# Attention pass of a graph layer: one load of each step's word per engine, and the words under way kept in registers

## The chip, the cores and the metric

The kernel runs on one core of a Trainium2 chip. The core has five engines that run side by side, each with a queue of instructions of its own: TensorE (PE, matrix products), VectorE (DVE), ScalarE (ACT), GpSimd (POOL) and SyncE (SP, which here only issues transfers). The metric is the device time of one launch in microseconds (us), the median of several.

## The reference, cut to what matters

The whole kernel computes two graph layers on 3125 nodes with 256 features and 50000 edges. The edges are sorted by their target `dst`. The change is in one stage of the first layer, the sum of softmax-weighted values over the edges of a node:

```python
# one row per edge, 4 heads of 64 features
ex  = exp(score - largest_score_of[dst])          # E x 4
num = segment_sum(ex[:, :, None] * v[src], dst)   # N x 4 x 64
den = segment_sum(ex, dst)                        # N x 4
rst = num / den
```

Scores, values of the edges' sources (stored in DRAM as `d_v`) and the largest scores have been made by stages before it.

## The kernel before, in words

Edges are held in tiles of 128 (one edge per partition), nodes in 25 tiles of 128. A list of steps, made at run time from `dst`, pairs a node tile `t` with two neighbouring edge tiles `i` and `i + 1` (`G = 2`) that hold edges of that node tile. A step is one 32-bit word in SBUF, `t << 9 | i` (`PACK = 9`). `step_at(eng, m, s)` loads the word of step `s` into a register of the engine `eng` (`value_load`, line 397) and takes `t` and `i` out of it; addresses that depend on `t` or `i` are worked out by register instructions of the engine's own queue.

`attention_sums` goes through the steps four at a time (`UN = 4` buffers, index `u`); such four steps are a round, and the loop is a `Fori` over rounds. There are 212 steps, so 53 rounds, the last of which stands unrolled behind the loop on ACT and DVE (`last` is the number of rounds in the loop). For step `s = 4 r + u`:

- SP waits until `weigh` of step `s - 4` is done and loads `v[:, u]`, 128 x 512 values (L759).
- ACT makes a one-hot matrix: `distance` writes |node number - dst| for both edge tiles (two `Abs` instructions of 128x128, L771), `one_hot` turns it into 0 and 1 (one `Relu` of 128x256, L777). `distance` of step `s + 1` is issued ahead of `one_hot` of step `s`. `one_hot` waits until PE has finished step `s - 4`.
- DVE `weigh` multiplies `v` with the edge's four weights (L822, 128x512). DVE `keep` adds the finished product of a step from PSUM to the node tile's row of `sums` (L832, 128x260). The order on DVE is `weigh(s + 2)`, `keep(s)`.
- POOL copies the weights themselves beside the weighted values, to be summed too (L806, 128x8); it waits for PE's step `s - 4`.
- PE multiplies one-hot and weighted values of the two edge tiles into PSUM (L863; an fp32 product of two tiles is four passes, so four MATMUL records per step).

So DVE runs two steps ahead of its own `keep`, and ACT, POOL and SP up to four steps ahead of PE. The order of the work is written out by hand with semaphores: `weighted`, `multiplied`, `kept`, `hots`, `copied`, `own`, `arrived[u]`. Both `weigh` and `keep` call `step_at` at their start, so that DVE loads the word of every step twice, two steps apart; ACT, POOL and SP load it once.

Of the kernel before, what the change touches and what calls it, by code (L numbers as in the profile page):

```python
# [11 lines left out]
ACT = mybir.ActivationFunctionType  # L12
AX = mybir.AxisListType

P = 128
# [379 lines left out]
def step_at(eng, m, s):  # L395

    v = eng.value_load(m.steps[0:1, bass.ds(s, 1)])
    why = "the steps are made of tiles that exist"
    t = eng.snap(eng.bass.s_assert_within(v >> PACK, 0, NT - 1, skip_runtime_bounds_check_because=why))
    i = eng.snap(eng.bass.s_assert_within(v & ((1 << PACK) - 1), 0, ET - G, skip_runtime_bounds_check_because=why))  # L400
    return t, i

def last_round(eng, m):
    return eng.value_load(m.rounds[0:1, 1:2], min_val=1, max_val=STEPS // UN - 1)

# [331 lines left out]
def attention_sums(nc, a, m, banks):  # L738

    WIDE = F + HEADS  # L740
    with Stage(nc, "attend") as st:
        v = st.sb("v", [P, UN, G, F])
        pv = st.sb("pv", [P, UN, G, WIDE])
        minus = st.sb("minus", [P, ET])
        far = st.sb("far", [P, UN, G * P])
        hot = st.sb("hot", [P, UN, G * P])
        weighted, multiplied, kept, hots, copied, own = (
            st.sem(x) for x in ("weighted", "multiplied", "kept", "hots", "copied", "own"))
        diff, exps, free = st.sem("diff"), st.sem("exps"), st.sem("free")
        arrived = [st.sem(f"arrived{u}") for u in range(UN)]  # L750
        with nc.Block() as block:
            @block.sync
            def _(sp):
                with sp.Fori(0, rounds_of(sp, m)) as r:
                    for u in range(UN):
                        t, i = step_at(sp, m, r * UN + u)
                        sp.wait_ge(weighted, r * UN + (u + 1))
                        sp.sem_inc(free, 1)
                        sp.dma_start(v[:, u], m.d_v[u][:, bass.ds(i, G), :]).then_inc(arrived[u], 16)  # L759

            @block.scalar
            def _(act):
                act.sem_inc(multiplied, UN)
                act.wait_ge(diff, 3)
                nc.scalar.activation(m.probs[:], m.probs[:], ACT.Exp, scale=float(HD) ** -0.5).then_inc(exps, 1)

                def distance(r, u):
                    t, i = step_at(act, m, r * UN + u)
                    act.wait_ge(hots, r * UN + (u + 1))
                    for g in range(G):  # L770
                        nc.scalar.activation(far[:, u, g * P:(g + 1) * P], m.node_no[:, bass.ds(t * P, P)], ACT.Abs,  # L771
                                             bias=minus[:, bass.ds(i + g, 1)]).then_inc(own, 1)

                def one_hot(r, u):
                    act.wait_ge(own, r * (UN * G) + (G * u + G))
                    act.wait_ge(multiplied, r * UN + (u + 1))
                    nc.scalar.activation(hot[:, u], far[:, u], ACT.Relu, scale=-1.0, bias=1.0).then_inc(hots, 1)  # L777
                last = last_round(act, m)
                t, i = step_at(act, m, 0)
                for g in range(G):  # L780
                    nc.scalar.activation(far[:, 0, g * P:(g + 1) * P], m.node_no[:, bass.ds(t * P, P)], ACT.Abs,
                                         bias=minus[:, bass.ds(i + g, 1)]).then_inc(own, 1)
                with act.Fori(0, last) as r:
                    for u in range(UN):
                        if u + 1 < UN:
                            distance(r, u + 1)
                        else:
                            distance(r + 1, 0)
                        one_hot(r, u)
                for u in range(UN):  # L790
                    if u + 1 < UN:
                        distance(last, u + 1)
                    one_hot(last, u)

            @block.gpsimd
            def _(pool):
                pool.sem_inc(hots, UN)
                pool.sem_inc(weighted, UN)
                pool.sem_inc(kept, UN)
                pool.wait_ge(exps, 1)  # L800
                with pool.Fori(0, rounds_of(pool, m)) as r:
                    for u in range(UN):
                        s = pool.snap(r * UN + u)
                        t, i = step_at(pool, m, s)
                        pool.wait_ge(multiplied, s + 1)
                        nc.gpsimd.tensor_copy(pv[:, u, :, F:WIDE], m.probs[:, bass.ds(i, G), :]).then_inc(copied, 1)  # L806

            @block.vector
            def _(dve):
                nc.vector.tensor_tensor(m.probs[:], m.scores[:].rearrange("p h j -> p j h"), m.probs[:],  # L810
                                        ALU.subtract).then_inc(diff, 1)
                dve.wait_ge(diff, 1)

                nc.vector.tensor_scalar(m.probs[:], m.probs[:], 0.0, None, ALU.min).then_inc(diff, 1)
                nc.vector.tensor_scalar(minus[:], m.dst[:], -1.0, None, ALU.mult).then_inc(diff, 1)
                dve.wait_ge(exps, 1)

                def weigh(r, u):
                    t, i = step_at(dve, m, r * UN + u)
                    dve.wait_ge(arrived[u], r * 16 + 16)  # L820
                    dve.wait_ge(multiplied, r * UN + (u + 1))
                    nc.vector.tensor_tensor(pv[:, u, :, 0:F].rearrange("p g (h d) -> p g h d", h=HEADS),  # L822
                                            v[:, u].rearrange("p g (h d) -> p g h d", h=HEADS),
                                            m.probs[:, bass.ds(i, G), :].unsqueeze(3).to_broadcast([P, G, HEADS, HD]),
                                            ALU.mult).then_inc(weighted, 1)

                def keep(r, u):
                    t, i = step_at(dve, m, r * UN + u)
                    dve.wait_ge(multiplied, r * UN + (u + 1 + UN))
                    dve.wait_ge(kept, r * UN + (u + UN))  # L830
                    at = m.sums[:, bass.ds(t, 1), :]
                    nc.vector.tensor_tensor(at, at, banks[u][:, 0:WIDE].unsqueeze(1), ALU.add).then_inc(kept, 1)  # L832
                last = last_round(dve, m)
                for u in range(2):
                    t, i = step_at(dve, m, u)
                    dve.wait_ge(arrived[u], 16)
                    nc.vector.tensor_tensor(pv[:, u, :, 0:F].rearrange("p g (h d) -> p g h d", h=HEADS),
                                            v[:, u].rearrange("p g (h d) -> p g h d", h=HEADS),
                                            m.probs[:, bass.ds(i, G), :].unsqueeze(3).to_broadcast([P, G, HEADS, HD]),
                                            ALU.mult).then_inc(weighted, 1)  # L840
                with dve.Fori(0, last) as r:
                    for u in range(UN):
                        if u + 2 < UN:
                            weigh(r, u + 2)
                        else:
                            weigh(r + 1, u + 2 - UN)
                        keep(r, u)
                for u in range(UN):
                    if u + 2 < UN:
                        weigh(last, u + 2)  # L850
                    keep(last, u)

            @block.tensor
            def _(pe):
                with pe.Fori(0, rounds_of(pe, m)) as r:
                    for u in range(UN):
                        s = pe.snap(r * UN + u)
                        pe.wait_ge(hots, s + (1 + UN))
                        pe.wait_ge(copied, s + 1)
                        pe.wait_ge(weighted, s + (1 + UN))  # L860
                        pe.wait_ge(kept, s + 1)
                        for g in range(G):
                            mm = nc.tensor.matmul(banks[u][:, 0:WIDE], hot[:, u, g * P:(g + 1) * P], pv[:, u, g],  # L863
                                                  start=g == 0, stop=g == G - 1)
                        mm.then_inc(multiplied, 1)
# [1486 lines left out]
```

## Time and profile before

| | |
|---|---|
| median of 3 runs | 4048.72 us (4047.67 to 4053.07) |
| profiled execution | 4048.99 us |
| its span | 4047.3 us |
| granted TensorE clock, mean of the span | 0.865 |
| busy share of the span | PE 77%, DVE 52%, ACT 29%, POOL 28% |
| attention pass, from the first transfer of `v` to the last `keep` | 860.9 to 1214.0 us |

The times of the table and of all rows come from the one profiled execution, except for the median. Line numbers such as L822 are those of the kernel before.
### The profile page before, as it was taken

What the parts mean: (1) busy time and instruction counts of PE and PEld (TensorE: products, weight loads), DVE (VectorE), ACT (ScalarE), POOL (GpSimd) and SP (SyncE); (2) the same over time, 40 slices, a digit from 0 to 9 for tenths busy, and PEclk for the clock granted to TensorE, in tenths of its full rate; (3) what the DMA queues carried; (4) which work ended last, traced back from release to release, by engine and by line L of the source; (5) the groups of instructions that cost most, each with busy time, mean ns of one, the idle gap of its engine ahead of it and who ended that gap; (6) DMA issues with size and microseconds to landing.
All of it is one profiled execution on the core that took longest, in us unless ns stands there. A gap on an engine that the chain in (4) does not pass through costs nothing. (4 is left out here: it accounts for less than half of the span.)

```text
span 4047.3 us, 64299 instructions
## 1 busy us (share of the span) xinstructions
PE 3103.2 (77%) x12404; PEld 2300.5 (57%) x12405; DVE 2122.8 (52%) x3755; ACT 1177.5 (29%) x2663; POOL 1118.4 (28%) x1227
## 2 busy tenths in 40 slices
PE   4767667736666734999998899999996868666979
PEld 2634434424445433567776788888885656554568
DVE  6466666666663286111113455555556874884231
ACT  1000000036662411233333000000007975653312
POOL 2166666601110000000000355555550001750023
PEclk9866665569998875799999999999998989887979
DMA  1588888835550000000000565556650000004134
GB/s 54 174 268 268 267 265 266 268 87 161 160 151 6 18 0 17 0 16 8 16 8 3 173 176 175 174 178 178 175 175 33 0 19 1 1 0 163 78 128 139
DMA packets 219248, 449.64 MB, mean 111 GB/s; under 512 B 30122, under 2 KB 109299, under 8 KB 217771
## 3 DMA queue, kind: packets, MB, share of 16 engines
q1 hardware_dynamic: 158762, 257.80, 20.7%
q0 software_dynamic: 60416, 190.96, 15.9%
q8 instruction: 39, 0.64, 0.1%
q14 instruction: 31, 0.25, 0.0%
HBM read 360.37 MB, written 89.26 MB: 111 GB/s over the span
## 5 line engine op out<-in xcount | busy, mean ns | idle before, releaser
L1401 POOL DMA_INDIRECT conv_h<-table_h,conv_ix x424 | 409.0, 965 | 1048.4 <-ACT conv_ix L1392 957.8
L1452 PE MATMUL bank<-conv_w,conv_eT 128*128 128x256 f32 x2532 | 580.9, 379 | 0.0
L489 PE MATMUL bank<-scores_k,scores_hotT 128*128 x848 | 391.1, 609 | 183.1 <-DVE scores_hotT L518 177.0
L1452 PEld LDWEIGHTS bank<-conv_w,conv_eT 128*128 128x128 f32 x2532 | 482.1, 190 | 64.5
L467 POOL DMA_INDIRECT scores_qv<-table_qv,scores_ix x424 | 400.9, 946 | 374.0 <-ACT scores_ix L457 160.8
L489 PEld LDWEIGHTS bank<-scores_k,scores_hotT 128*128 128x128 f32 x848 | 225.6, 294 | 331.2 <-issue 299.0
L1351 DVE SCALAR_TENSOR_TENSOR x<-bank,soft_w,x 128x256 f32 x200 | 96.8, 484 | 443.2 <-PE bank L1285 443.2
L863 PE MATMUL bank<-attend_pv,attend_hot 128*128 128x260 f32 x848 | 237.2, 403 | 118.9 <-POOL attend_pv L806 83.0
L1313 ACT ACTIVATE soft_h<-bank,soft_bi,soft_sc 128x320 f32<-128x320 f32 x320 | 197.5, 617 | 340.0 <-PE bank L1278 340.0
L1392 ACT ACTIVATE conv_ix<-src 128x2 int32 x212 | 43.2, 204 | 770.1 <-DVE conv_msg L1426 736.6
L863 PEld LDWEIGHTS bank<-attend_pv,attend_hot 128*128 128x128 f32 x848 | 145.2, 190 | 210.8 <-POOL attend_pv L806 121.9
L1459 PE MATMUL bank<-conv_msg,conv_hot 128*128 128x256 f32 x848 | 223.3, 386 | 44.5 <-DVE conv_msg L1426 44.5
L457 ACT ACTIVATE scores_ix<-src 128x2 int32 x212 | 43.1, 203 | 666.2 <-DVE scores_qk L525 584.6
L525 DVE TENSOR_TENSOR scores_qk<-scores_qv,bank 128x512 f32<-128x512 f32 x212 | 145.7, 687 | 135.7 <-DMA scores_qv<-table_qv,scores_ix 89.8
L1459 PEld LDWEIGHTS bank<-conv_msg,conv_hot 128*128 128x128 f32 x848 | 157.0, 190 | 84.6 <-DVE conv_msg L1426 64.6
L822 DVE TENSOR_TENSOR attend_pv<-attend_v,probs 128x512 f32<-128x512 f32 x210 | 145.5, 693 | 102.4 <-issue 99.1
L167 PE MATMUL bank<-ident,rows 128*128 128x128 f32 x250 | 51.1, 362 | 192.4 <-DVE rows L156 190.8
L1278 PE MATMUL bank<-xT,soft_W 128*128 x640 | 188.4, 444 | 8.0 <-issue 3.7
L1421 DVE TENSOR_TENSOR conv_be<-bank,conv_b 128x512 f32<-128x512 f32 x212 | 145.9, 688 | 91.4 <-PE bank L1452 86.6
L1278 PE MATMUL bank<-soft_h,soft_W 128*128 128x320 f32 x640 | 182.4, 438 | 0.0
L1285 PE MATMUL bank<-soft_W,soft_h 128*128 128x256 f32 x800 | 179.2, 379 | 0.0
L771 ACT ACTIVATE attend_far<-node_no,attend_minus 128x128 f32 x422 | 146.3, 394 | 77.9 <-ACT attend_hot L777 77.6
(420 smaller groups left out, 5250.8 us busy)
## 6 DMA issues: line engine op xcount, KB each, us to landing
conv_eT<-in_edges SPq DMA_DIRECT2D x212, 384.0 KB, 3.3
edge_v<-scores_qv SPq DMA_DIRECT2D x212, 256.0 KB, 4.2
attend_v<-edge_v SPq DMA_DIRECT2D x212, 256.0 KB, 2.7
hidden_rows<-rows SPq DMA_DIRECT2D x25, 512.0 KB, 3.8
top_wd<-in_top_wd SPq DMA_DIRECT2D x8, 1024.0 KB, 11.4
scores_qv<-table_qv,scores_ix POOLq DMA_INDIRECT x424, 4.8
conv_h<-table_h,conv_ix POOLq DMA_INDIRECT x424, 3.3
table_qv<-qkv_rows SPq DMA_DIRECT2D x50, 128.0 KB, 1.7
```

The costliest lines, as they stand in the source:

```text
L467: nc.gpsimd.indirect_dma_start(out=qv[:, u, g - u * G, :], out_offset=None, in_=m.d_qv, in_offset=bass.IndirectOffsetOnAxis(ap=ix[:, g:g + ...
L489: mm = nc.tensor.matmul(banks[u][:, g * F:(g + 1) * F], hotT[:, u, g * P:(g + 1) * P], k[:, bass.ds(t, 1), :].rearrange("p t f -> p (t f)" ...
L525: nc.vector.tensor_tensor(qk[:, u % 2].rearrange("p (g f) -> p g f", g=G), qv[:, u, :, 0:F], banks[u][:, 0:G * F].rearrange("p (g f) -> p ...
L771: nc.scalar.activation(far[:, u, g * P:(g + 1) * P], m.node_no[:, bass.ds(t * P, P)], ACT.Abs, bias=minus[:, bass.ds(i + g, 1)]).then_inc( ...
L863: mm = nc.tensor.matmul(banks[u][:, 0:WIDE], hot[:, u, g * P:(g + 1) * P], pv[:, u, g], start=g == 0, stop=g == G - 1)
L1278: mm = nc.tensor.matmul(banks[k % HSLOTS][:, 0:CW], W[:, j, layer, f, c * P:(c + 1) * P], cols, start=f == 0, stop=f == FT - 1)
L1285: mm = nc.tensor.matmul(banks[HSLOTS + u][:, 0:F], h2[:, f, u * P:(u + 1) * P], W[:, j, 2, f], start=f == 0, stop=f == FT - 1)
L1313: nc.scalar.activation(dst[:, c, hf * CW:(hf + 1) * CW], banks[k % HSLOTS][:, 0:CW], ACT.Relu, scale=sc[:, layer, bass.ds(e, 1), c], bias= ...
L1401: nc.gpsimd.indirect_dma_start(out=h[:, u, g, :], out_offset=None, in_=m.d_h, in_offset=bass.IndirectOffsetOnAxis(ap=ix[:, u * G + g:u * G ...
L1421: nc.vector.tensor_tensor(be[:, u % 2], banks[u][:, 0:G * F].rearrange("p (g f) -> p g f", g=G), b[:].unsqueeze(1).to_broadcast([P, G, F]) ...
L1452: mm = nc.tensor.matmul(banks[u][:, g * F:(g + 1) * F], eT[:, u, g, c], w[:, c], start=c == 0, stop=c == EC - 1)
L1459: mm = nc.tensor.matmul(acc(u), hot[:, u, g], msg[:, u, g], start=g == 0, stop=g == G - 1)
```

## The change

On ACT and DVE `step_at` gives way to three small functions: `word_at` loads a word, `node_tile` and `edge_tile` take `t` and `i` out of a word that is already in a register.

- On DVE the word of a step is loaded once, three steps before its `keep`, between the `weigh` of another step and the `keep` that follows. Three words are under way; at the end of a round they are copied to three registers that live across the loop's branch (`reg_mov`), and at its start they are read back (`snap`).
- On ACT the load of the next step's word moves from ahead of `distance` to between the two `Abs` instructions of a `distance`. `distance` is called once per edge tile and takes `t` and `i` out of the word each time. One word is carried across the branch.
- The order of `weigh`, `keep`, `distance` and `one_hot`, and all semaphores, stay as they were. SP, POOL and PE are untouched.

```diff
+def word_at(eng, m, s):
+    return eng.value_load(m.steps[0:1, bass.ds(s, 1)])
+
+def node_tile(eng, v):
+    return eng.snap(eng.bass.s_assert_within(v >> PACK, 0, NT - 1, ...))
+
+def edge_tile(eng, v):
+    return eng.snap(eng.bass.s_assert_within(v & ((1 << PACK) - 1), 0, ET - G, ...))
...
-                def distance(r, u):
-                    t, i = step_at(act, m, r * UN + u)
-                    act.wait_ge(hots, r * UN + (u + 1))
-                    for g in range(G):
-                        nc.scalar.activation(far[:, u, g * P:(g + 1) * P], ...)
+                def distance(word, u, g):
+                    t, i = node_tile(act, word), edge_tile(act, word)
+                    nc.scalar.activation(far[:, u, g * P:(g + 1) * P], ...)
...
+                def round_of(r, word, more):
+                    for u in range(UN):
+                        if more or u + 1 < UN:
+                            act.wait_ge(hots, r * UN + (u + 2))
+                            distance(word, (u + 1) % UN, 0)
+                            later = word_at(act, m, r * UN + (u + 2)) if more or u + 2 < UN else word
+                            distance(word, (u + 1) % UN, 1)
+                            word = later
+                        one_hot(r, u)
+                    return word
...
                 with act.Fori(0, last) as r:
-                    for u in range(UN):
-                        if u + 1 < UN:
-                            distance(r, u + 1)
-                        else:
-                            distance(r + 1, 0)
-                        one_hot(r, u)
+                    act.reg_mov(carried, round_of(r, act.snap(carried), True))
...
-                def weigh(r, u):
-                    t, i = step_at(dve, m, r * UN + u)
+                def weigh(r, u, word):
+                    i = edge_tile(dve, word)
...
-                def keep(r, u):
-                    t, i = step_at(dve, m, r * UN + u)
+                def keep(r, u, word):
+                    t = node_tile(dve, word)
...
+                def round_of(r, words, more):
+                    for u in range(UN):
+                        if u + 2 < UN:
+                            weigh(r, u + 2, words[u + 2])
+                        elif more:
+                            weigh(r + 1, u + 2 - UN, words[u + 2])
+                        if more or u + 3 < UN:
+                            words.append(word_at(dve, m, r * UN + (u + 3)))
+                        keep(r, u, words[u])
+                    return words[UN:]
...
                 with dve.Fori(0, last) as r:
+                    for x, word in zip(carried, round_of(r, [dve.snap(x) for x in carried], True)):
+                        dve.reg_mov(x, word)
```

## Rows read from the trace of the kernel before

**Rows 1.** Stage view of the whole pass (PE, PEld, DVE, ACT, POOL busy, clock, DMA).
```profile
860.89:1214.03 353.14, 237.17 (x848) 145.17 (x848) 237.12 (x427) 234.34 (x638) 64.53 (x212) 0.99 0.58 157
```

**Rows 2.** Who waited for whom, 880 to 1200 us (total us, times, longest).
```profile
POOL attend_pv L806 <- PE bank L863: 260.4, 195, 1.4
...
DVE attend_pv L822 <- issue: 93.7, 193, 0.8
...
ACT attend_hot L777 <- PE bank L863: 23.2, 49, 0.5
DVE attend_pv L822 <- PE bank L863: 1.6, 2, 0.8
```

**Rows 3.** Timeline of DVE, one round (start us, duration us).
```profile
1000.35 0.69 DVE L822 TENSOR_TENSOR attend_pv<-attend_v,probs 128x512 f32<-128x512 f32 x1 [0.80 <-issue]
1001.13 0.43 DVE L832 TENSOR_TENSOR sums<-sums,bank 128x260 f32 x1
1001.85 0.69 DVE L822 TENSOR_TENSOR attend_pv<-attend_v,probs 128x512 f32<-128x512 f32 x1 [0.29 <-issue]
...
1003.59 0.69 DVE L822 TENSOR_TENSOR attend_pv<-attend_v,probs 128x512 f32<-128x512 f32 x1 [0.54 <-issue]
1004.26 0.43 DVE L832 TENSOR_TENSOR sums<-sums,bank 128x260 f32 x1
1005.00 0.69 DVE L822 TENSOR_TENSOR attend_pv<-attend_v,probs 128x512 f32<-128x512 f32 x1 [0.31 <-issue]
1005.67 0.43 DVE L832 TENSOR_TENSOR sums<-sums,bank 128x260 f32 x1
1006.89 0.69 DVE L822 TENSOR_TENSOR attend_pv<-attend_v,probs 128x512 f32<-128x512 f32 x1 [0.80 <-issue]
```

**Rows 4.** Line L397 on DVE's sequencer, 880 to 1200 us (ns min/median/max).
```profile
L397 DVEq TENSOR_LOAD <-steps x391: 298/302/327, 879.8 to 1199.5; - x196
L397 DVEq FUSED_REGOPS  x244: 53/53/75, 882.4 to 1199.4; - x122
```

**Rows 5.** Line L397 on DVE, starts between 1006.17 and 1006.18 us.
```profile
L397 DVEq TENSOR_LOAD <-steps x1: 300/300/300, 1006.2 to 1006.2; - x1
```

**Rows 6.** Line L820 on DVE, starts between 1006.50 and 1006.51 us.
```profile
L820 DVEq FUSED_REGOPS  x1: 60/60/60, 1006.5 to 1006.5; - x1
```

**Rows 7.** Line L841, DVE's loop over rounds, the whole pass.
```profile
L841 DVEq COMPARE_BRANCH  x52: 50/56/69, 874.6 to 1209.1; - x52
L841 DVEq MOVE  x1: 36/36/36, 867.1 to 867.1; - x1
```

**Rows 8.** Timeline of DVE, the end of the last round.
```profile
1212.24 0.42 DVE L832 TENSOR_TENSOR sums<-sums,bank 128x260 f32 x1
1212.92 0.42 DVE L832 TENSOR_TENSOR sums<-sums,bank 128x260 f32 x1 [0.26 <-DVE sums L832]
```

**Rows 9.** Timeline of ACT at the start of the pass.
```profile
866.22 0.39 ACT L771 ACTIVATE attend_far<-node_no,attend_minus 128x128 f32 x1
866.51 0.40 ACT L777 ACTIVATE attend_hot<-attend_far 128x256 f32<-128x256 f32 x1
866.95 0.69 ACT L771 ACTIVATE attend_far<-node_no,attend_minus 128x128 f32 x2
867.54 0.40 ACT L777 ACTIVATE attend_hot<-attend_far 128x256 f32<-128x256 f32 x1
...
868.55 0.40 ACT L777 ACTIVATE attend_hot<-attend_far 128x256 f32<-128x256 f32 x1
```

**Rows 10.** Line L397 on ACT, starts between 866.27 and 866.28 us.
```profile
L397 ACTq TENSOR_LOAD <-steps x1: 283/283/283, 866.3 to 866.3; - x1
```

**Rows 11.** Line L771, the distances, 880 to 1200 us.
```profile
L771 ACTq FUSED_REGOPS  x588: 37/54/85, 880.0 to 1199.9; - x196
L771 ACTq ALU_OP  x196: 38/38/38, 880.1 to 1199.7; - x196
```

**Rows 12.** Line L759, the transfers of v, 880 to 1200 us.
```profile
L759 SPq DMA_DIRECT2D attend_v<-edge_v x196: 332/333/338, 880.0 to 1199.6; - x196
...
DMA to landing us min/median/max: 2.6/2.7/2.9
```

**Rows 13.** PE's passes alone, two stretches (us, PE busy, clock, DMA share, GB/s).
```profile
867.28:870.35 3.07, 3.06 (x7) 0.52 0.40 102
870.35:872.30 1.95, 1.95 (x10) 1.00 0.68 242
```

**Rows 14.** Timeline of PE, the step behind the weigh at 1001.85.
```profile
1002.65 1.11 PE L863 MATMUL bank<-attend_pv,attend_hot 128*128 128x260 f32 x4 [0.39 <-issue]
```

**Rows 15.** POOL's copy and DVE's weigh by line, 880 to 1200 us.
```profile
L806 POOL COPY attend_pv<-probs x195: 189/191/509, 881.2 to 1199.2; 128x8 f32 x195
L822 DVE TENSOR_TENSOR attend_pv<-attend_v,probs x195: 691/693/694, 880.5 to 1198.6; 128x512 f32<-128x512 f32 x195
```

More of the change, by code:

```diff
@@ L401, in step_at @@
     return t, i
+def word_at(eng, m, s):
+    return eng.value_load(m.steps[0:1, bass.ds(s, 1)])
+def node_tile(eng, v):
+    return eng.snap(eng.bass.s_assert_within(v >> PACK, 0, NT - 1,
+                                             skip_runtime_bounds_check_because="the steps are made of tiles that exist"))
+def edge_tile(eng, v):
+    return eng.snap(eng.bass.s_assert_within(v & ((1 << PACK) - 1), 0, ET - G,
+                                             skip_runtime_bounds_check_because="the steps are made of tiles that exist"))
 def last_round(eng, m):
@@ L765, in _ @@
                 nc.scalar.activation(m.probs[:], m.probs[:], ACT.Exp, scale=float(HD) ** -0.5).then_inc(exps, 1)
-                def distance(r, u):
-                    t, i = step_at(act, m, r * UN + u)
-                    act.wait_ge(hots, r * UN + (u + 1))
-                    for g in range(G):
-                        nc.scalar.activation(far[:, u, g * P:(g + 1) * P], m.node_no[:, bass.ds(t * P, P)], ACT.Abs,
-                                             bias=minus[:, bass.ds(i + g, 1)]).then_inc(own, 1)
+                def distance(word, u, g):
+                    t, i = node_tile(act, word), edge_tile(act, word)
+                    nc.scalar.activation(far[:, u, g * P:(g + 1) * P], m.node_no[:, bass.ds(t * P, P)], ACT.Abs,
+                                         bias=minus[:, bass.ds(i + g, 1)]).then_inc(own, 1)
                 def one_hot(r, u):
@@ L777, in one_hot @@
                     nc.scalar.activation(hot[:, u], far[:, u], ACT.Relu, scale=-1.0, bias=1.0).then_inc(hots, 1)
-                last = last_round(act, m)
[L779 to L782, printed above, removed]
-                with act.Fori(0, last) as r:
-                    for u in range(UN):
-                        if u + 1 < UN:
-                            distance(r, u + 1)
-                        else:
-                            distance(r + 1, 0)
-                        one_hot(r, u)
[L790 to L793, printed above, removed]
+                def round_of(r, word, more):
[8 more added lines that the diff above has]
+                    return word
+                last = last_round(act, m)
+                carried = act.alloc_register("attend_word")
+                word = word_at(act, m, 0)
+                distance(word, 0, 0)
+                act.reg_mov(carried, word_at(act, m, 1))
+                distance(word, 0, 1)
+                with act.Fori(0, last) as r:
+                    act.reg_mov(carried, round_of(r, act.snap(carried), True))
+                round_of(last, act.snap(carried), False)
             @block.gpsimd
@@ L832, in keep @@
                     nc.vector.tensor_tensor(at, at, banks[u][:, 0:WIDE].unsqueeze(1), ALU.add).then_inc(kept, 1)
[L833 to L840, printed above, removed]
@@ L841, in _ @@
-                with dve.Fori(0, last) as r:
+                def round_of(r, words, more):
                     for u in range(UN):
                         if u + 2 < UN:
[L844 to L851, printed above, removed]
+                            weigh(r, u + 2, words[u + 2])
[5 more added lines that the diff above has]
+                    return words[UN:]
@@ new lines, in _ @@
+                last = last_round(dve, m)
+                carried = [dve.alloc_register(f"attend_word{k}") for k in range(3)]
+                for k in range(3):
+                    word = word_at(dve, m, k)
+                    dve.reg_mov(carried[k], word)
+                    if k < 2:
+                        i = edge_tile(dve, word)
+                        dve.wait_ge(arrived[k], 16)
+                        nc.vector.tensor_tensor(pv[:, k, :, 0:F].rearrange("p g (h d) -> p g h d", h=HEADS),
+                                                v[:, k].rearrange("p g (h d) -> p g h d", h=HEADS),
+                                                m.probs[:, bass.ds(i, G), :].unsqueeze(3).to_broadcast([P, G, HEADS, HD]),
+                                                ALU.mult).then_inc(weighted, 1)
@@ L853, in _ @@
+                with dve.Fori(0, last) as r:
+                    for x, word in zip(carried, round_of(r, [dve.snap(x) for x in carried], True)):
+                        dve.reg_mov(x, word)
+                round_of(last, [dve.snap(x) for x in carried], False)
             @block.tensor
```

## Prediction

> **What bounds the kernel now.** Only the attention pass is touched, so I read that stage alone: 353.1 us of the span [rows 1]. In the stage view the reader is to see that no engine is full there: PE 237, DVE 237, ACT 234 us busy, the transfers at 0.58 of the DMA engines, the clock at 0.99. Something that is not counted as busy sets the pace.
>
> Next the waits [rows 2]. POOL waits for PE in every step and ACT in some, because both may only be four steps ahead; that is slack. DVE is the odd one: 193 of 195 times its `weigh` came after an idle time that ends in "issue", and only twice did it wait for PE. DVE waits for its own sequencer.
>
> The timeline of DVE [rows 3] shows where. `weigh` to `weigh` over a round is 1000.35 to 1006.89, 6.54 us, and the loop's branches give the same mean: 1209.1 - 874.6 over 51 rounds, 6.56 us [rows 7]. The two instructions of a step last 0.69 and 0.43, four times 4.48 us, so over 2 us a round are sequencer. From `weigh` to the next `keep` it is 0.78 in one step and 0.67 in another; from `keep` to `weigh` 0.72 and 0.74, and 1.22 over the branch (1005.67 to 1006.89). DVE loads 391 words in the 320 us, eight a round, 0.302 us each [rows 4]. From the start of a load to that of the next instruction it is 0.33 us (1006.17 to 1006.50) [rows 5, 6], and that next instruction, L820, works out a wait value and does not need the word: the sequencer stands still for a load, whoever needs it. With the longer cases I take 0.34.
>
> **The change on DVE, part by part.**
>
> Removed: four of eight loads a round, 4 x 0.34 = 1.36 us. They are those ahead of `weigh`, where little covers them: from `keep` to `weigh` the sequencer needs 0.72, the engine only the 0.43 of `keep`. Without the load 0.72 becomes about 0.3 of sequencer and some 0.4 of engine.
>
> Also removed: part of the five FUSED_REGOPS a round (244 in 49 rounds) that work out the word's address [rows 4]. Such an instruction costs 0.1 us with its gap: the `weigh` to `keep` of 0.78 has one, that of 0.67 (1003.59 to 1004.26) has none, as its step number was worked out for `weigh` already. Four loads at new step numbers want about four of them, so one goes: 0.1 us (bounds 0 and 0.2).
>
> Added: three `reg_mov` and three `snap` a round. The nearest row is the loop's MOVE, 0.036 us [rows 7]; with the gap of 0.035 that stood behind the load above, 0.07 each. Six of them are 0.43; if register instructions are merged, as the many FUSED_REGOPS suggest, or the `snap` is only a name, it is one or two instructions, 0.12. I take 0.3. They stand beside the branch, where nothing covers them.
>
> Kept: the other four loads, behind `weigh`, with waits and addresses as they were, so 0.78 from `weigh` to `keep`.
>
> Does the engine become the bound? A pair is then 0.78 + 0.3 = 1.08 of sequencer and 0.69 + 0.43 = 1.12 of engine by records, less by starts: `weigh` to `keep` came at 0.67, shorter than the 0.69 of `weigh`, so instructions overlap a little. They are equal, and can share a surplus only if the sequencer may run ahead of its engine. On ACT it does: a load starts at 866.27 while the `Relu` that stands ahead of it starts only at 866.51 [rows 9, 10]. I take the same for DVE. If not, the three short passages cost max(0.3, 0.4), 0.1 each, 0.3 a round.
>
> Sum per round of the loop: 1.36 + 0.1 - 0.3 = 1.16 us less, so 6.56 becomes 5.4. Bounds: 1.36 + 0.2 - 0.12 = 1.44 above, 1.36 - 0.43 - 0.3 = 0.63 below. There are 52 such rounds [rows 7]. The last round, outside the loop, loses five of six loads, but its end hangs on PE's last step: `keep` to `keep` is 0.68 there with a load in it [rows 8], and I count 0.6 us for all of it. Total 52 x 1.16 + 0.6 = 61 us.
>
> **What else must keep up with 5.4 us a round (1.35 a step).**
>
> PE: at full clock ten passes start in 1.95 us, 0.195 to 0.22 each, so a step of four is 0.9 [rows 13].
>
> The chain from `weigh` over PE to `keep`: `weigh` at 1001.85, PE at 1002.65, its end at 1003.76 [rows 3, 14], and 0.2 until `keep` runs: 2.1 us. `keep` comes two steps and 0.78 behind its `weigh`, at least 2 x 1.08 + 0.78 = 2.9. It fits.
>
> SP and the transfers: 0.58 of the DMA engines at 353/212 = 1.67 a step is 0.97 us of transfer a step. A transfer lands 2.7 us after its issue [rows 12]; `weigh` 0.69, some 0.3 of SP's registers before the issue, 2.7 and 0.25 of DVE's registers are 3.95 us, and the buffer comes round every 5.4. SP's own step is the issue 0.333 [rows 12] plus a load and six small ones, about 1.1 us by an estimate from these. It fits, with the DMA share near 0.71.
>
> ACT: the load between two `Abs` is covered no better than before, and `t` and `i` are taken out twice. Where nothing held it, at the start of the pass, a step took 1.03 and 1.01 us (866.51, 867.54, 868.55) [rows 9], though in the pass it takes 1.64. The second unpacking costs at most an address instruction of 0.085 and an ALU_OP of 0.038 with their gaps [rows 11], 0.2 a step; one `reg_mov`, one `snap` and the branch add some 0.4 a round. So 4 x 1.22 + 0.4 = 5.3 at worst, 4.5 at best. It hides behind DVE, but at worst with only 0.1 to spare.
>
> Prediction: 4048.99 of the profiled execution less 61 is 3988.0; against the median, 0.3 lower than that execution, also 3988 within what I can tell.
>
> **The rivals.**
>
> A. *The same mechanism, with a smaller gain*: DVE's sequencer does not run ahead, all six moves stand, or ACT becomes the bound. For it: ACT's worst sum of 5.3 is close to 5.4, and one more address instruction per `Abs` would pass it. Against: rows 9 show ACT with a large reserve. The gain is then 0.5 to 1.0 a round: 3997 to 4022.
>
> B. *GpSimd's copy gets in the way of `weigh`.* In the rows `weigh` always takes 691 to 694 ns, while the copy stretches from 189 to 509 ns [rows 15]: when both meet, so far the copy waits. Its place in the round is set by PE's end, and that will shift; if the copy starts just ahead of `weigh` in each step and `weigh` must wait for all of it, that is 0.19 a step, 4 x 0.19 = 0.76 a round, 40 us: 3988 + 40 = 4028. Against: the copy waits for PE's end, and would have to meet `weigh` at its worst in each of four uneven steps. The Trainium skill, page "SBUF — State Buffer", section "SBUF: two separate sides", says that a VectorE instruction with two SBUF inputs and a GpSimd instruction that reads SBUF hold one pair of ports exclusively, whoever starts first; the stretched copies agree with the one half of it, and that `weigh` could be the one that waits no row here shows.
>
> C. *Slower: PE at half clock.* The pass begins cold: seven passes take 3.07 us at a clock of 0.52, 0.44 each [rows 13], so 1.75 a step, and 7.0 a round is over the 6.56 of today. Were the clock low for the whole pass, the time would be 4049 + 52 x 0.45 = 4072. It decides from the point where PE's step passes 1.64. Against: PE will have less idle time than now, 237 us busy in some 292 rather than in 353, and today it holds 0.99. The clock rose within the first round.
>
> D. *The change does nothing*: were the sequencer not what DVE waits for, or the added instructions worth as much as the loads (1.46 a round, twenty moves). Rows 2 speak against it.
>
> **How the numbers follow.** The forecast, DVE bound by its sequencer with 1.0 to 1.44 a round gained, gets 0.70: 3974 to 3997. A gets 0.17 (3997 to 4022), B 0.03 (about 4028), C 0.04, D 0.03, and a gain above my upper bound, such as fewer address instructions, 0.03. The range 3974 to 4010 holds the forecast's 0.70 and about 0.12 of A. Faster is the forecast, A, B and the last case, 0.93. A measurement of this kernel can tell some 0.2%, 8 us, from no change; within that is D, 0.03; slower is C, 0.04.
>
> **What would show each step.** In the profile after: about 196 loads on DVE's sequencer in 320 us x 5.4/6.56, four a round instead of eight; the branch on DVE every 5.4 us; `keep` to `weigh` at 0.4 rather than 0.72, and some 1.15 over the branch; `weigh` to `keep` unchanged near 0.78; the pass 61 us shorter and the rest of the span as before; DMA share about 0.7. Wrong would be: `weigh` waiting for PE or for the transfer of `v` instead of "issue", a `one_hot` of ACT that comes after PE was ready (then A), a `weigh` longer than 0.7 (B), or a round that is longer across the branch than 1.3 (moves dearer than I priced them).

## The result, and the profile after

The changed kernel takes 3982.11 us (median of 4, 3979.87 to 3983.54) against 4048.19 us on the same chip: the ratio is 0.9834, with a 95% interval of 0.9817 to 0.9851. The forecast was 3988 with a range of 3974 to 4010. The profiled execution took 3981.72 us, its span is 3979.7.

The stage view of the pass answers to [rows 1] (us, then PE, PEld, DVE, ACT, POOL busy, clock, DMA share, GB/s):

```profile
857.04:1140.98 283.94, 237.92 (x848) 145.92 (x848) 229.46 (x427) 227.46 (x637) 48.92 (x212) 0.98 0.69 196
```

The same work is done in 283.9 rather than 353.1 us: 69.2 us less. The span is 67.6 us shorter, so all of the gain arose in the pass and nearly all of it arrived at the end. PE is now busy for 84% of the pass and the transfers take 0.69 of the DMA engines.

Who waited for whom, 880 to 1120 us, answers to [rows 2]:

```profile
POOL attend_pv L824 <- PE bank L890: 199.1, 185, 1.4
...
DVE attend_pv L840 <- issue: 26.7, 46, 0.6
ACT attend_hot L790 <- PE bank L890: 21.5, 46, 0.5
DVE sums L850 <- PE bank L890: 8.5, 47, 0.2
```

Before, DVE was idle ahead of `weigh` in 193 of 195 steps; now it is in 46 of 184, once a round, across the branch. The other idle time has moved ahead of `keep` and is 0.2 us, also once a round. The row puts it down to PE. One such `keep` stands at 1004.85 in the timeline of DVE below; it takes the product of the `weigh` at 1001.72, which PE began at 1002.51, and a step of PE lasts 1.1 us [rows 14]. PE had been done for a microsecond; the sequencer was late there. PE's timeline, 1000 to 1006 us:

```profile
1002.51 3.93 PE L890 MATMUL bank<-attend_pv,attend_hot 128*128 128x260 f32 x13 [0.62 <-POOL attend_pv L824]
```

The timeline of DVE over one round (start, duration) answers to [rows 3]:

```profile
1001.72 0.69 DVE L840 TENSOR_TENSOR attend_pv<-attend_v,probs 128x512 f32<-128x512 f32 x1 [0.58 <-issue]
1002.51 0.43 DVE L850 TENSOR_TENSOR sums<-sums,bank 128x260 f32 x1
1002.85 0.68 DVE L840 TENSOR_TENSOR attend_pv<-attend_v,probs 128x512 f32<-128x512 f32 x1
1003.57 0.42 DVE L850 TENSOR_TENSOR sums<-sums,bank 128x260 f32 x1
1003.98 0.69 DVE L840 TENSOR_TENSOR attend_pv<-attend_v,probs 128x512 f32<-128x512 f32 x1
1004.85 0.42 DVE L850 TENSOR_TENSOR sums<-sums,bank 128x260 f32 x1 [0.18 <-PE bank L890]
1005.20 0.69 DVE L840 TENSOR_TENSOR attend_pv<-attend_v,probs 128x512 f32<-128x512 f32 x1
1005.93 0.43 DVE L850 TENSOR_TENSOR sums<-sums,bank 128x260 f32 x1
```

`keep` to `weigh` is 0.34 and 0.41 where it was 0.72 and 0.74; so `weigh` starts before `keep`, 0.43 long, has ended. `weigh` to `keep` is 0.72 to 0.87. The step at 1003.98 is the one that PE seems to hold up: its 0.87 is 0.08 to 0.15 us more than that of the others. The kernel before had a passage of that kind too, ahead of its `weigh` at 1003.59 (idle 0.54 where others have 0.29 and 0.31) [rows 3], at another place of the round. In both traces a register instruction follows the one before it 0.11 us later there than the same instruction does in the other steps. I have no cause for it.

The sequencer's loads of words and their address instructions, 880 to 1120 us, answer to [rows 4, 7] (ns min/median/max, first and last start):

```profile
L406 DVEq FUSED_REGOPS  x184: 53/53/53, 880.1 to 1119.1; - x184
L406 DVEq TENSOR_LOAD <-steps x184: 297/304/325, 880.1 to 1119.2; - x184
```

and its loop over rounds, the whole pass:

```profile
L875 DVEq FUSED_REGOPS  x52: 170/170/210, 863.8 to 1131.8; - x52
L875 DVEq COMPARE_BRANCH  x52: 50/56/69, 870.5 to 1136.8; - x52
```

```profile
L877 DVEq FUSED_REGOPS  x52: 142/142/142, 870.3 to 1136.6; - x52
```

There are 184 loads in 240 us where there were 391 in 320, so one a step instead of two. A round is (1136.8 - 870.5) / 51 = 5.22 us; it was 6.56. The six register copies of the change are not six instructions either. They are in two: the loop's FUSED_REGOPS behind the branch has grown from 85 to 170 ns, and ahead of the branch the `reg_mov` line, L877, has one of 142 ns where the kernel before had an ALU_OP of 40. The kernel before had:

```profile
L841 DVEq FUSED_REGOPS  x52: 85/85/99, 867.2 to 1202.8; - x52
L841 DVEq ALU_OP  x52: 40/40/40, 874.5 to 1209.0; - x52
```

The traces say directly that the sequencer is the pace. DVE's queue has 42 sequencer instructions a round before and 36 after. Over 47 rounds each of them follows the one before it at a distance that changes by less than 0.03 us from round to round, waits on semaphores included, and these distances add up to 6.56 and 5.22 us: the sequencer never stands for another engine.

### The profile page after: what moved, and what is told of

It reads as the page before. It is cut to its first block and busy times, and to the rows that moved or that the text cites. A ratio compares the mean times of both kernels' runs of the same rounds, so it can differ in the third digit from the quotient of the medians.

```text
span 3979.7 us, 63982 instructions
## 1 busy us (share of the span) xinstructions
PE 3093.8 (78%) x12404; PEld 2291.7 (58%) x12405; DVE 2113.0 (53%) x3755; ACT 1170.5 (29%) x2663; POOL 1102.5 (28%) x1227
## 5 line engine op out<-in xcount | busy, mean ns | idle before, releaser
L504 PE MATMUL bank<-scores_k,scores_hotT 128*128 x848 | 378.5, 592 | 191.4 <-DVE scores_hotT L533 186.0
L784 ACT ACTIVATE attend_far<-node_no,attend_minus 128x128 f32 x424 | 168.3, 397 | 24.3 <-ACT attend_hot L790 7.8
L1312 PEld LDWEIGHTS bank<-soft_W,soft_h 128*128 128x128 f32 x800 | 152.0, 190 | 24.9
```

The source lines that it names most:

```text
L504: mm = nc.tensor.matmul(banks[u][:, g * F:(g + 1) * F], hotT[:, u, g * P:(g + 1) * P], k[:, bass.ds(t, 1), :].rearrange("p t f -> p (t f)" ...
L1312: mm = nc.tensor.matmul(banks[HSLOTS + u][:, 0:F], h2[:, f, u * P:(u + 1) * P], W[:, j, 2, f], start=f == 0, stop=f == FT - 1)
```

## The experiments

All ran on three other chips than the result, where the kernel before takes 4225.6 to 4232.7 us. The other stages are slower there and the pass is not: with the old DVE queue ("ACT part alone") the pass takes 353.2 us, what stands ahead of it 126 us more than in the profile before, and what stands behind it 57 us more. So I compare ratios to the kernel before, and rounds from the traces. A round is taken from the row of DVE's loop branch, which stands with each experiment but two: its last start less its first, over 51. (For "two loads, one unused" it is 994.3 to 1260.6, for the first "no second wait" 999.5 to 1249.2.)

| kernel | ratio to before, 95% interval | round, us |
|---|---|---|
| DVE part alone | 0.9839 (0.9810 to 0.9869) | 5.22 |
| ACT part alone | 0.9992 (0.9977 to 1.0006) | 6.56 |
| load behind `keep` | 0.9845 (0.9817 to 0.9873) | 5.23 |
| two loads, one unused | 0.9848 (0.9816 to 0.9880) | 5.22 |
| two used loads | 1.0006 (0.9991 to 1.0020) | 6.75 |
| ACT with two loads | 0.9977 (0.9966 to 0.9987) | 6.34 |
| DVE without loads | 0.9787 (0.9771 to 0.9804) | 4.70 |
| changed kernel again | 0.9843 (0.9819 to 0.9867) | 5.22 |
| no second wait | 0.9785 (0.9768 to 0.9801) | 4.90 |
| no second wait, again | 0.9796 (0.9775 to 0.9818) | 4.90 |

### Which part of the change

The new DVE queue with ACT's queue as it was (`distance(r, u)` with `step_at`), and the other way round:

```diff
 # DVE part alone: scalar block of the kernel before, vector block of the changed one
...
-                    act.reg_mov(carried, round_of(r, act.snap(carried), True))
+                    for u in range(UN):
+                        if u + 1 < UN:
+                            distance(r, u + 1)
+                        else:
+                            distance(r + 1, 0)
+                        one_hot(r, u)
...
```

> The new DVE queue with the old ACT queue. Theory (DVE's sequencer alone sets the pace): the whole gain, 3982 us within 3, and a round of 5.2 us as in the changed kernel. Rival (ACT's moved load has a share, or ACT with its load ahead of the distances is too slow for 5.2 us a round): at least 8 us above 3982.

> The new ACT queue with the old DVE queue. Theory: no change against the kernel before, 4048 us within 4, a round of 6.56 us on DVE. Rival (ACT's part gives some of the 66 us): below 4040.

The loop branch of DVE, with DVE's part alone:

```profile
L872 DVEq COMPARE_BRANCH  x52: 50/56/69, 1000.2 to 1266.4; - x52
```

and with ACT's part alone:

```profile
L859 DVEq COMPARE_BRANCH  x52: 50/56/69, 1000.7 to 1335.2; - x52
```

DVE's part has the whole gain (0.9839, a round of 5.22), ACT's has none (0.9992, 6.56). Both are as the theory had it, and ACT's old order keeps up with 5.22 us a round as well.

### Does it matter where the load stands?

The load goes from behind `weigh` to behind `keep`:

```diff
-                        if more or u + 3 < UN:
-                            words.append(word_at(dve, m, r * UN + (u + 3)))
                         keep(r, u, words[u])
+                        if more or u + 3 < UN:
+                            words.append(word_at(dve, m, r * UN + (u + 3)))
```

> As the changed kernel, but DVE loads the word after keep, behind its shorter instruction (0.43 us), instead of after weigh, behind its longest (0.69 us). Theory (the sum of the sequencer's work sets the pace, and the sequencer runs ahead of its engine, so the place of a load doesn't matter): 3982 us within 5. Rival (a load costs what its cover leaves over): weigh to keep 0.67 and keep to weigh 0.71 us, 0.6 to 0.8 us a round more, 4012 to 4022 us.

DVE's loop branch:

```profile
L875 DVEq COMPARE_BRANCH  x52: 50/56/69, 995.1 to 1261.8; - x52
```

0.9845, a round of 5.23: no difference. The timeline of its DVE shows how:

```profile
1100.53 0.69 DVE L840 TENSOR_TENSOR attend_pv<-attend_v,probs 128x512 f32<-128x512 f32 x1 [0.74 <-issue]
1101.14 0.42 DVE L850 TENSOR_TENSOR sums<-sums,bank 128x260 f32 x1
1101.61 0.69 DVE L840 TENSOR_TENSOR attend_pv<-attend_v,probs 128x512 f32<-128x512 f32 x1
1102.22 0.42 DVE L850 TENSOR_TENSOR sums<-sums,bank 128x260 f32 x1
1102.80 0.69 DVE L840 TENSOR_TENSOR attend_pv<-attend_v,probs 128x512 f32<-128x512 f32 x1 [0.16 <-issue]
1103.41 0.42 DVE L850 TENSOR_TENSOR sums<-sums,bank 128x260 f32 x1
```

`weigh` to `keep` is now 0.61 each time, as short as the engine allows (no pair comes closer than 0.60 in any timeline here), and `keep` to `weigh` 0.47 and 0.58. The rival would have had 0.67 and 0.71. The sequencer had `keep` queued while `weigh` ran and went on to the load: the load for the step at 1101.61 starts at 1102.06, and the `keep` queued ahead of it only at 1102.22. So the surplus of one passage was spent in the next. "Behind its longest operation" is not what makes the change good; one load less a step is.

### What a load costs

The first try loaded the word twice in a row and left the second value unused:

```diff
                             words.append(word_at(dve, m, r * UN + (u + 3)))
+                            word_at(dve, m, r * UN + (u + 3))
```

> As the changed kernel, but DVE loads the same word twice in a row behind weigh; the second value is not used. Theory (a load stops the sequencer for 0.34 us, and the gap from weigh to keep is already the sequencer's): four times 0.34 us a round, in 52 rounds 71 us more, 4053 us, about the time before. Rival (what stands behind weigh is covered by its 0.69 us): less than 20 us more, under 4002 us.

Measured: 0.9848 (0.9816 to 0.9880). This looks like the rival, but says nothing, since the row of its loads over the whole pass shows one a step:

```profile
L406 DVEq TENSOR_LOAD <-steps x212: 297/305/321, 986.1 to 1261.3; - x106
```

The unused load was not in the program that ran; the run is the changed kernel again. So both loads had to be used:

```diff
                             words.append(word_at(dve, m, r * UN + (u + 3)))
-                        keep(r, u, words[u])
+                        keep(r, u, word_at(dve, m, r * UN + u))
```

> As the changed kernel, but keep's own word is loaded once more behind weigh, and keep uses that one: two loads in a row, both used, behind the 0.69 us of weigh. Theory (a load stops the sequencer for 0.34 us, and from weigh to keep the sequencer is already the longer one): 4 x 0.34 to 4 x 0.44 us a round more, so the pass is 71 to 90 us longer than the changed kernel's and the time is at or up to 0.5% above that of the kernel before. Rival (loads behind weigh are covered): the ratio stays at 0.984.

DVE's loop branch:

```profile
L875 DVEq COMPARE_BRANCH  x52: 50/56/69, 991.3 to 1335.4; - x52
```

1.0006, a round of 6.75: the gain is gone, with the new order of the queue kept and the loads given back. Two more things differ from the changed kernel, though, in opposite directions. There are seven address instructions a round instead of four, and fewer copies, since the carried words of two steps are no longer used; the loop's lines have

```profile
L875 DVEq MOVE  x53: 36/36/44, 984.0 to 1329.0; - x53
```

```profile
L877 DVEq FUSED_REGOPS  x52: 58/58/58, 991.2 to 1335.3; - x52
```

instead of the 170 and 142 ns, and a FUSED_REGOPS of 55 ns beside them. The difference in the round is 6.75 - 5.22 = 1.53 us, 0.38 a load with all this in it. Added up from start to next start, the loads alone take 2.73 us a round here and 1.36 in the changed kernel: 0.34 each, in both. The timeline:

```profile
1101.59 0.68 DVE L840 TENSOR_TENSOR attend_pv<-attend_v,probs 128x512 f32<-128x512 f32 x1
1102.74 0.43 DVE L850 TENSOR_TENSOR sums<-sums,bank 128x260 f32 x1 [0.47 <-issue]
```

`weigh` to `keep` is 1.15 with two loads between them, 0.43 more than at 1002.85 of the changed kernel. Two loads behind the longest operation are not hidden by it. (Here `weigh` across the branch is put down to PE, 44 times in 300 us. DVE's sequencer instructions still follow each other without a wait, so PE is named wrongly here too, as at 1004.85 above.)

### A wait less

`weigh(s + 2)` waits for PE's step `s - 2`, though `keep(s - 2)`, earlier on the same queue, has waited for it:

```diff
                     dve.wait_ge(arrived[u], r * 16 + 16)
-                    dve.wait_ge(multiplied, r * UN + (u + 1))
```

> As the changed kernel, but weigh doesn't wait for PE: keep of the step before it on the same queue has waited for a later value of the same semaphore already. Theory (the sequencer's sum sets the pace): four instructions of 0.045 us with their gaps fall away, 4 x 0.08 = 0.3 us a round, 16 us less than the changed kernel, a ratio near 0.980. Rival (DVE itself or PE is by now as slow as the sequencer): no change, 0.984.

0.9785 and a round of 4.90: 0.32 us less a round, or 17 us in 52. By the medians it was 26 us less than the changed kernel as it ran with the unused load on another chip, more than the pass can give, so I ran it once more, with the changed kernel on the same chip.

> The changed kernel itself, beside the next run on one chip. Theory: a pass of 283.5 us and a round of 5.22 us whatever the chip, as the pass hangs on a queue of instructions and not on the memory; the ratio to the kernel before is 0.983 to 0.985.

> The changed kernel without weigh's wait for PE, once more, now beside the changed kernel. Theory: its pass is 16.7 us shorter than the changed kernel's (266.8 us, a round of 4.9 us), and so is the time: 0.4% less, a ratio of 0.979 to 0.981 to the kernel before. What the first run showed beyond that (26 us less than another kernel's time) was chance outside the pass.

DVE's loop branch in the changed kernel, and then without the second wait:

```profile
L875 DVEq COMPARE_BRANCH  x52: 50/56/69, 990.5 to 1256.9; - x52
```

```profile
L874 DVEq COMPARE_BRANCH  x52: 50/56/69, 999.6 to 1249.4; - x52
```

4150.70 us for the changed kernel and 4137.57 without the wait, 13 us less, where the traces have (5.224 - 4.898) x 52 = 17 us: the same within what the intervals allow. This version computes the same and beats both kernels.

### What comes after DVE's sequencer

DVE goes round with its first three words and loads none. Its weights and node tiles are then those of the first steps, and the instructions that do the work are the same:

```diff
-                            words.append(word_at(dve, m, r * UN + (u + 3)))
+                            words.append(words[u])
```

> As the changed kernel, but DVE loads no words in the loop: it goes round with the three words of the first steps, so weights and node tiles are wrong. Its sequencer's sum falls by 4 x 0.43 us, to 3.5 us a round. Theory (SP's queue is next, at 1.16 us a step by its records): a round of 4.7 us, 30 us less than the changed kernel, ratio near 0.977. Rivals: ACT is next, at 4.4 to 5.3 us a round, so -43 to 0 us; or the transfers are, at 0.97 us a step, 3.9 us a round, -69 us, ratio 0.967.

DVE's loop branch:

```profile
L875 DVEq COMPARE_BRANCH  x52: 50/56/69, 981.7 to 1221.6; - x52
```

A round of 4.70, as SP's instructions add up to. The waits of this kernel, 1000 to 1200 us:

```profile
DVE attend_pv L840 <- DMA attend_v<-edge_v: 22.7, 53, 0.7
...
DVE attend_pv L840 <- PE bank L890: 4.2, 21, 0.3
DVE attend_pv L840 <- issue: 2.6, 15, 0.2
ACT attend_hot L790 <- PE bank L890: 0.4, 2, 0.2
```

`weigh` now waits for its values in 53 cases, at a DMA share of only 0.74, with transfers that land 3.0 us after their issue as in the changed kernel: it is the issue that is late, not the transfer. And the issue is late because SP's own queue is full. In the changed kernel SP stands up to 0.59 us at its wait for `weigh`; here the instruction there (an ALU_OP at L772) is followed by the next after 0.07 to 0.08 us every time, and the distances from start to start add up to 4.71 us a round with no wait among them. ACT is close behind: its `one_hot` hardly waits by the table above (0.4 us), but its sequencer still stands some 0.3 us a round ahead of `one_hot`. The ratio, 0.9787, is no better than that without the second wait; the trace has (5.22 - 4.70) x 52 = 27 us less in the pass, and its four times spread over 30 us (4117 to 4147), so here I go by the trace.

### ACT's reserve

ACT loads the word of the step a second time, for its second distance:

```diff
-                            distance(word, (u + 1) % UN, 1)
+                            distance(word_at(act, m, r * UN + (u + 1)), (u + 1) % UN, 1)
```

> As the changed kernel, but ACT loads the word of a step a second time for the second of its two distances: one load more a step, 4 x 0.31 to 4 x 0.38 us a round. ACT waits for PE about 0.7 us a round in the changed kernel. Theory (ACT has a reserve of about 0.7 us a round and then becomes the bound): ACT's round is 5.75 to 6.1 us, 28 to 46 us more than the changed kernel, a ratio of 0.991 to 0.995. Rival (ACT has a large reserve, as its start of the pass suggested): no change, 0.984.

DVE's loop branch:

```profile
L875 DVEq COMPARE_BRANCH  x52: 50/56/69, 1006.4 to 1329.5; - x52
```

The round is 6.34, the ratio 0.9977: ACT has become the bound, as the theory had it, though by more than it said (5.75 to 6.1). Here it is ACT's sequencer instructions, 51 a round, that follow one another without a wait and add up to 6.35 us. ACT's timeline there:

```profile
1101.70 0.40 ACT L784 ACTIVATE attend_far<-node_no,attend_minus 128x128 f32 x1 [0.51 <-issue]
1102.01 0.40 ACT L790 ACTIVATE attend_hot<-attend_far 128x256 f32<-128x256 f32 x1
1102.31 0.39 ACT L784 ACTIVATE attend_far<-node_no,attend_minus 128x128 f32 x1
1103.20 0.40 ACT L784 ACTIVATE attend_far<-node_no,attend_minus 128x128 f32 x1 [0.51 <-issue]
```

A step takes 1.50 us, 0.51 of it idle between the two distances, behind the two loads. What I had not counted is that a word in a new register must be unpacked anew. By the distances from start to start the second load and its unpacking add 0.50 us a step. Taken off four times, this leaves 6.34 - 2.0 = 4.3 us for ACT's own round in the changed kernel (an estimate), 0.9 below the 5.22 and 0.4 below SP's 4.70.

## Why the prediction was right, step by step

- **What bounds the pass.** DVE's sequencer: shown. Only DVE's part moves the time, the loads given back take all of it away again, a wait less gains what its instruction costs (0.08 us each), and the distances between the sequencer's instructions add up to the round, before and after.
- **Loads, 4 x 0.34 = 1.36 us a round.** Right: by starts 2.74 us a round before and 1.36 after, 1.38 less. The run with two used loads has 2.73 again.
- **Address instructions, 0.1.** Right: five a round before [rows 4], four after (184 in 46 rounds), 0.12 us less by starts.
- **Moves, 0.3: too dear, within the bounds.** From start to next start the instruction behind the branch (L875) takes 0.23 us where it took 0.13, and the one ahead of it (L877) 0.18 where the ALU_OP of L841 took 0.07: the six copies cost 0.20 us, between my bounds of 0.12 and 0.43. They were merged, as the prediction held possible. With the measured terms the sum is 1.38 + 0.12 - 0.20 = 1.30 a round; measured 6.56 - 5.22 = 1.34. The last 0.04 are small differences among the other register instructions. So the loads were right almost to the digit, and most of the 8 us by which the pass came out shorter than forecast (69.2 for 61) is the 0.1 that I overpriced, times 52. The 0.6 us for the last round did not show.
- **The sequencer runs ahead of DVE.** Taken over from ACT's rows in the prediction, shown here by the load behind `keep`.
- **`keep` to `weigh` 0.4, 1.15 over the branch.** Measured 0.34 to 0.41 and 1.01 (a `keep` at 1000.71, the `weigh` at 1001.72). The 0.34 is as close as any `weigh` follows a `keep` in these timelines but for 0.33 in the run without loads; of the 0.14 less over the branch, 0.1 is the copies' price.
- **What else must keep up.** PE, the chain over PE and the transfers did. SP's 1.1 us a step was right, and its round of 4.70 is the next bound. For ACT the second unpacking that I counted (0.2 us a step) did not come: line L784 has three address instructions and one ALU_OP a step, exactly as L771 had [rows 11]:

```profile
L784 ACTq FUSED_REGOPS  x552: 37/57/85, 880.0 to 1119.4; - x184
...
L784 ACTq ALU_OP  x184: 38/38/38, 880.2 to 1118.9; - x184
```

- **Rival A (ACT becomes the bound, smaller gain)** is refuted for this kernel. One load and one unpacking more a step (0.50 us), and ACT decides; its own round has some 0.9 us to spare.
- **Rival B (GpSimd's copy in the way of `weigh`)** did not show. `weigh` takes 682 to 694 ns; the copy still stretches, to 349 at most in these 240 us. Once a round a copy now starts 0.13 us ahead of a `weigh`, the order that I had priced, and that `weigh` takes no longer than 0.69. Their rows by line, 880 to 1120 us, answer to [rows 15]:

```profile
L824 POOL COPY attend_pv<-probs x185: 189/191/349, 879.8 to 1119.9; 128x8 f32 x185
```

```profile
L840 DVE TENSOR_TENSOR attend_pv<-attend_v,probs x184: 682/689/694, 880.1 to 1118.9; 128x512 f32<-128x512 f32 x184
```

  In the kernel without the second wait the copy happens to start just ahead of a `weigh` once a round. POOL and DVE there:

```profile
1100.25 0.19 POOL L824 COPY attend_pv<-probs 128x8 f32 x1 [1.35 <-PE bank L889]
```

```profile
1100.26 0.72 DVE L839 TENSOR_TENSOR attend_pv<-attend_v,probs 128x512 f32<-128x512 f32 x1
...
1101.47 0.69 DVE L839 TENSOR_TENSOR attend_pv<-attend_v,probs 128x512 f32<-128x512 f32 x1
```

  That `weigh` lasts 0.72 instead of 0.69. All 41 `weigh` of that pass that last longer than 0.695 us start 0.01 to 0.04 us behind a copy; the 51 that start 0.05 to 0.10 behind one last 0.684 to 0.686, and where the copy starts less than about 0.01 ahead, the copy lasts 0.74 and `weigh` 0.69. So the direction of the rival exists, but its price is at most 0.04 us and not the 0.19 of the whole copy that I had put in: by these rows `weigh` is held until about 0.05 us after the copy's start. The Trainium skill, page "SBUF — State Buffer", section "SBUF: two separate sides", has whoever starts second blocked for the whole of the first instruction; the copy's stretching to 0.74 us agrees, the 0.03 us do not. No run was made for this alone.
- **Rival C (half clock)** did not show: 0.98 over the pass. **Rival D (no change)** is refuted by the ratio of 0.9834 and by the run with DVE's part alone.
- **Outside the pass** the span changed by 1.5 us: the pass begins 3.9 us earlier (857.0 for 860.9), and from its end to that of the span it is 2838.7 us where it was 2833.3. That code is untouched; what shifts it was not tried.

## What to carry to other kernels

When an engine idles with "issue" as the reason, add up its sequencer's instructions by start times over one loop, and compare with the engine's own time: the larger sum is the pace, and the place of an instruction in the queue matters little as long as the sequencer can run ahead. Where the sequencer is the pace, a load of a register costs its full 0.34 us wherever it stands, so carry the word in a register rather than look for a place to hide the load; carrying three words cost 0.20 us a round against the 1.38 of four loads. Then look at waits that an earlier wait on the same queue already covers: each is an instruction too.

## What the runs showed of the hardware that I had not expected

- Six register copies around a loop's branch went into two fused register instructions (85 to 170 ns behind the branch, 142 ns for a 40 ns ALU_OP ahead of it) and cost 0.20 us a round together.
- DVE starts a 128x260 instruction 0.61 us after the start of a 0.69 us one, and a 128x512 one 0.34 us after the start of a 0.43 us one: some 0.08 us of each record lies under the next.
- A load that is not needed by the next instruction still holds DVE's sequencer for 0.34 us, and 36 to 42 sequencer instructions a round set the pace of an engine that is busy for 4.3 to 4.5 us of a round of 5.2 to 6.6.
- One step of a round has 0.11 us more in DVE's sequencer than the others with like instructions, in the kernel before and after, at different places. Its cause stays open.
- A VectorE instruction with two inputs in SBUF that starts 0.01 to 0.04 us behind a 128x8 copy of GpSimd lasts 0.70 to 0.72 us instead of 0.68 to 0.69; one that starts 0.05 us or more behind it is not held. When the copy starts less than about 0.01 us ahead, it is the copy that waits: 0.74 us instead of 0.19.
